# Cross-attention and routed attention: the high part of the routed rows written by VectorE, the product repeated on GpSimd

## The reference

```
x = x + xattn(layernorm(x), ctx)                  # 8 heads, 77 context rows
rw = gating(layernorm(x))                         # 16 weights per token
q, k, v = sum_e rw[t, e] * (x @ {q,k,v}_proj[e])
attn = softmax(causal(q k^T / 8)) v
mixed = attn[:, :, None, :] * rw[..., None]
x = x + einsum('bted,edc->btc', mixed, o_proj)
```

## Time and profile before

| | |
|---|---|
| median of 3 runs | 2802.98 us |
| the profiled execution's own time | 2805.71 us |
| its span, first to last instruction | 2803.8 us |
| busy share of the span: PE, PEld, DVE, ACT, POOL | 96%, 92%, 87%, 36%, 42% |
| mean granted TensorE clock | 0.991 |

### The profile page before, as it was taken

How to read it: one execution, slowest core, us unless ns; L and a number is a source line. 1 busy time by engine, 2 the same in 40 slices (tenths; PEclk the granted TensorE clock), 3 DMA queues, 4 the chain that set the end, 5 groups by cost and what they waited for, 6 DMA issues and landing times.

```text
span 2803.8 us, 64494 instructions
## 1 busy us (share of the span) xinstructions
PE 2702.4 (96%) x19012; PEld 2581.8 (92%) x19012; DVE 2439.1 (87%) x6755; ACT 1020.0 (36%) x2448; POOL 1190.0 (42%) x1739
## 2 busy tenths in 40 slices
PE   5999999999999999999999999999999999999996
PEld 4999999999999999999999999999999999999996
DVE  6898888888888888988988889888889889888884
ACT  3343333333333333433333333333334334333331
POOL 1343443444444434434434434444344344344343
PEclk8999999999999999999999999999999999999998
DMA  4111111111111111111111111111111111111111
GB/s 103 29 45 44 32 44 35 40 44 28 44 48 28 44 44 31 44 44 31 44 39 36 44 30 41 48 28 44 44 31 44 44 31 44 43 32 44 35 36 39
DMA packets 131435, 113.58 MB, mean 41 GB/s; under 512 B 24720, under 2 KB 130640, under 8 KB 131408
## 3 DMA queue, kind: packets, MB, share of 16 engines
q1 hardware_dynamic: 131408, 113.23, 16.5%
HBM read 95.38 MB, written 17.83 MB: 40 GB/s over the span
## 4 chain that ended last, share of the span: by engine, by line
PE 73%; DVE 12%; issue 9%; ACT 4%; POOL 1%; DVEq 1%; POOLq 0%; DMA 0%; ACTq 0%; SPq 0%
PE bank_b L373 9%; PE bank_b L374 8%; PE bank_a L375 8%; PE bank_b L375 8%; PE bank_a L374 8%; PE bank_a L373 8%; PE bank_c L373 4%; PE bank_c L375 4%; PE bank_c L374 4%; PE bank_a L485 4%; DVE acc L996 3%; DVE acc L993 2%; DVE mix L1037 1%; PE bank_a L445 1%; DVE s_max L923 1%
## 5 line engine op out<-in xcount | busy, mean ns | idle before, releaser
L373 PE MATMUL bank_b<-wqkv_hi,x2T_lo 128*128 128x384 f32 (+1 forms) x2048 | 726.4, 355 | 34.3 <-DVE acc L996 33.7
L374 PE MATMUL bank_b<-wqkv_lo,x2T_hi 128*128 128x384 f32 (+1 forms) x2048 | 693.5, 339 | 0.0
L375 PE MATMUL bank_b<-wqkv_hi,x2T_hi 128*128 128x384 f32 (+1 forms) x2048 | 688.8, 336 | 0.0
L996 DVE SCALAR_TENSOR_TENSOR acc<-bank_b,rw,acc 128x192 f32<-128x192 f32 x1792 | 641.6, 407 | 5.3 <-PE bank_b L375 2.9
L1252 POOL TENSOR_TENSOR mixs_lo<-mix,mixs_hi 128x512 fp32r<-128x512 f32 x256 | 379.9, 1514 | 153.7 <-ACT mixs_hi L772 153.7
L373 PEld LDWEIGHTS bank_b<-wqkv_hi,x2T_lo 128*128 128x128 f32 x2048 | 385.8, 188 | 57.5 <-DVE acc L996 53.6
L374 PEld LDWEIGHTS bank_b<-wqkv_lo,x2T_hi 128*128 128x128 f32 x2048 | 386.2, 189 | 0.0
L375 PEld LDWEIGHTS bank_b<-wqkv_hi,x2T_hi 128*128 128x128 f32 x2048 | 385.1, 188 | 0.0
L1174 POOL TENSOR_TENSOR pow_out<-pow_in,expo 128x2 f32<-128x2 f32 (+1 forms) x128 | 111.7, 873 | 596.4 <-DVE pow_in L853 509.3
L373 PE MATMUL bank_c<-wo_hi,mixs_lo 128*128 128x256 f32 x1024 | 293.9, 287 | 3.7 <-POOL mixs_lo L1252 3.7
L375 PE MATMUL bank_c<-wo_hi,mixs_hi 128*128 128x256 f32 x1024 | 288.0, 281 | 0.0
(11 more groups left out here) (196 smaller groups left out, 6991.1 us busy)
## 6 DMA issues: line engine op xcount, KB each, us to landing
rw_all<-rw_dram SPq DMA_DIRECT2D x128, 512.0 KB, 5.7
xt<-in_x_dram SPq DMA_DIRECT2D x64, 256.0 KB, 2.7
out_dram<-mix SPq DMA_DIRECT2D x64, 256.0 KB, 2.2
ct<-in_ctx_dram SPq DMA_DIRECT2D x64, 57.8 KB
ct<-in_ctx_dram SPq DMA_DIRECT2D x64, 19.2 KB
mix<-in_L_ffn_o_proj_dram SPq DMA_DIRECT2D x2, 512.0 KB, 4.2
rw_dram<-rwT SPq DMA_DIRECT2D x64, 16.0 KB, 1.4
x_tiles<-in_L_xattn_Wq_dram SPq DMA_DIRECT2D x1, 512.0 KB, 6.9
```

Source lines behind the costliest of these rows:

```text
L373: nc.tensor.matmul(dst, lhs[1], rhs[0], start=start, stop=False)
L374: nc.tensor.matmul(dst, lhs[0], rhs[1], start=False, stop=False)
L375: return nc.tensor.matmul(dst, lhs[0], rhs[0], start=False, stop=stop)
L996: V.scalar_tensor_tensor(acc[:, t, k, :], src, rw[:, t, e:e + 1], acc[:, t, k, :], ALU.mult, ALU.add).then_inc(b_evac, 1)
```

## The change

DVE writes the product straight into the rounded tile `mixs[0]`, so that its output is the high part. ACT's copy goes. POOL makes the same product again, in float32, into `mix`, waits for its own product and for DVE's, and subtracts as before. The semaphores follow: `mix_ready` is now POOL's, `mix_hi` is DVE's; SP's reload of `rw_all` and ACT's next write of `aT2` wait for both readers; DVE waits, before it overwrites `mixs[0]`, for the last output product of the batch before; the wait for the store of `y` moves from DVE to POOL.

```diff
--- before.py
+++ after.py
@@ -326,6 +326,7 @@
                 sp.wait_ge(rwT_out, 16 * (n + 1))
                 if not (known(n) and n == 0):
                     sp.wait_ge(mix_ready, at(4, n - 1, 3))
+                    sp.wait_ge(mix_hi, at(4, n - 1, 3))
                 for k in range(2):
                     sp.dma_start(rw_all[k * D:(k + 1) * D, :, :],
                                  rw_dram[:, :].rearrange("(a k) t -> k a t", k=2)[k].partition_broadcast(D)).then_inc(rw_all_in, 16)
@@ -765,11 +766,10 @@
 
             def c_pv(n):
                 act.wait_ge(c_fill, c_at(n, C_PV))
+                if not (known(n) and n == 0):
+                    act.wait_ge(mix_ready, at(4, n - 1, 3))
+                    act.wait_ge(mix_hi, at(4, n - 1, 3))
                 nc.scalar.activation(aT2[:, :], bank_c(C_PV)[:, 0:T], copy).then_inc(aT2_ready, 1)
-
-            def c_mix(n, j):
-                act.wait_ge(mix_ready, at(4, n, j))
-                nc.scalar.activation(mixs[0][:, 2 * j:2 * j + 2, :], mix[:, 2 * j:2 * j + 2, :], copy).then_inc(mix_hi, 1)
 
             def step(i):
                 ahead, now, before, earlier = i + 1, i, i - 1, i - 2
@@ -779,7 +779,6 @@
                         fn(n, *k)
                         later(split_weights, fn.__name__.replace("exp", "s"), n, *k)
 
-                do(earlier, c_mix, 3)
                 do(now, a_exp, 1)
                 do(now, a_exp, 2)
                 do(now, a_exp, 3)
@@ -804,10 +803,7 @@
                 do(now, b_exp)
                 do(before, c_pT)
                 do(before, c_pv)
-                do(before, c_mix, 0)
                 do(ahead, a_exp, 0)
-                do(before, c_mix, 1)
-                do(before, c_mix, 2)
 
             for i in range(-1, 3):
                 step(i)
@@ -1032,10 +1028,10 @@
             def c_mix(n, j):
                 dve.wait_ge(rw_all_in, 32 * (n + 1))
                 dve.wait_ge(aT2_ready, at(1, n, 0))
-                if j == 3 and not (known(n) and n == 0):
-                    dve.wait_ge(y_out, 16 * n)
-                V.tensor_tensor(mix[:, 2 * j:2 * j + 2, :], rw_all[:, 2 * j:2 * j + 2, :],
-                                aT2[:, :].unsqueeze(1).to_broadcast([P, 2, T]), ALU.mult).then_inc(mix_ready, 1)
+                if j == 0 and not (known(n) and n == 0):
+                    dve.wait_ge(c_fill, c_at(n - 1, C_Y))
+                V.tensor_tensor(mixs[0][:, 2 * j:2 * j + 2, :], rw_all[:, 2 * j:2 * j + 2, :],
+                                aT2[:, :].unsqueeze(1).to_broadcast([P, 2, T]), ALU.mult).then_inc(mix_hi, 1)
 
             def c_y(n):
                 dve.wait_ge(c_fill, c_at(n, C_Y))
@@ -1248,6 +1244,13 @@
                                 ALU.mult).then_inc(p_ready, 1)
 
             def c_mix(n, j):
+                pool.wait_ge(rw_all_in, 32 * (n + 1))
+                pool.wait_ge(aT2_ready, at(1, n, 0))
+                if j == 3 and not (known(n) and n == 0):
+                    pool.wait_ge(y_out, 16 * n)
+                G.tensor_tensor(mix[:, 2 * j:2 * j + 2, :], rw_all[:, 2 * j:2 * j + 2, :],
+                                aT2[:, :].unsqueeze(1).to_broadcast([P, 2, T]), ALU.mult).then_inc(mix_ready, 1)
+                pool.wait_ge(mix_ready, at(4, n, j))
                 pool.wait_ge(mix_hi, at(4, n, j))
                 G.tensor_tensor(mixs[1][:, 2 * j:2 * j + 2, :], mix[:, 2 * j:2 * j + 2, :],
                                 mixs[0].bitcast(F32)[:, 2 * j:2 * j + 2, :], ALU.subtract).then_inc(mix_lo, 1)
```

## The result

| | before | after |
|---|---|---|
| median of the runs | 2803.93 us (4 runs, 2802.65 to 2807.08) | 3137.93 us (4 runs, 3137.86 to 3139.62) |
| span of the profiled execution | 2803.8 us | 3137.8 us |
| mean granted TensorE clock | 0.991 | 0.956 |

The ratio is 1.119, 95% interval 1.117 to 1.121: 334 us slower. The forecast was 3086 us with a range of 3010 to 3175.

The account below looks back on a forecast made before the run. PE, busy 96%, was taken as the bound, with POOL just in time for it. 276 us for 62 steps plus 2 and 5 at the end gave 283 us on the 2803.0 median: 3086 us, range 3010 to 3175.

Parts of the forecast that it names:

- POOL's chain sets the transposes: POOL's products, own waits and subtractions form one strict chain ahead of `a_p`, whose transposes PE then starts late.
- The chain's length: From `aT2` to POOL's last subtraction: eight instructions of 1.30 us, own waits and DVE's turns, 12.55 us instead of 7.75.
- rival 2: POOL's multiply is cheaper than `a_xb`, 1.01 us for 512 elements: 69 us less, 3017 us; chance 0.07.
- The transposes 4.45 us later: PE starts `a_pT` 0 at 1449.2 instead of 1444.72; the step pays all of it.
- rival 1: Granted clock falls in PE's new stops, some 3 us each: 3273 us every step, 3149 one in three; chance 0.2.
- The steps: The 62 steps in which mixes are followed by an `a_p` each pay 4.45 us: 276 us.
- The ends: The last two mixes, with no `a_p` behind them: 5 us in the last step, 2 us in the one before.
- The signs: POOL idle below 0.5 us before the mix, PE waiting 4 to 5 us for POOL, step about 47 us.
- The sign for rival 1: A granted clock below 0.95 in the steady steps would show that the clock falls in PE's stops.
- Waits and the rounded write costed at nothing: New waits of SP, ACT, DVE and POOL cost nothing; DVE's rounded write keeps the same 692 ns.
- rival 3: Not slower: POOL's chain ends within 8.1 us, in time for `a_pT`, 2803 us; chance 0.02.
- rival 4: DVE takes fewer turns against POOL than laid out: up to 1.4 us less per step, 2999 us; chance 0.04.

## Why the prediction was right, point by point

**POOL's chain sets the transposes: right, and measured from both sides.** Taking the product out removes all of the loss, halving it leaves 89 us.

**The chain's length: 12.55 us forecast, 12.28 seen.** The product on POOL alone takes 1.28 to 1.31 us, as the row of `a_xb` said, so rival 2 (a multiply of 1.01 us) is out, and so is the estimate of 1.11 us by the Trainium skill, page "GPSIMD Engine Reference", section 3.1. The order of turns came out as laid out; only the wait for DVE's first two products was split, 0.70 us ahead of POOL's first subtraction and 0.3 within it, which took 1.58. DVE's turns cost 1.65 us, where I had 1.95; that is the difference.

**The transposes 4.45 us later: 4.41 seen**, by 15.19 against 10.78 us. Some 0.2 of these are the clock (the last two pairs of quarter 1 at half rate), so the chain alone is 4.2.

**The clock: the term that was missing from the sum.** I kept the clock at its level in the forecast and gave its fall 0.2. It falls in every step but the third, so the event of rival 1 came, at a third of its price: the level of 1.2 GHz lasts some 3.4 us ((1.00 - 0.59) and (1.00 - 0.55) of two us each, over 0.50), not 7. Some 0.4 us of it lie in the stop itself. The last two pairs of quarter 1 take 1.44 us instead of 0.71, but with the stops filled PE waits 0.2 us for `a_p` at this place and starts the transposes only 0.2 us sooner, so only 0.2 of that counts. The transposes pay 0.78. Together that is 1.0 us, and by the run with the stops filled 0.9 per step, 58 us in all, where rival 1 had 186 for every step.

My reading of the earlier trace rows was the weak point. I put the new stretch between one of 0.52 and one of 0.82 us of work in two. But the 0.7 us were over 3.3 us, which is thinner than both; and what came was 0.97 us of work in the two us ahead of the fall, more than in the row of 0.82, behind which the clock had stayed up. So the work in two us did not sort these cases.

**The range: met in part by luck.** I drew its upper end for a fall in one step of three at 3 us each. It fell in nearly all of them at 0.9, and the sum stayed inside. The forecast was 3086 us; the chain makes 14 less, the clock 58 more, the ends 3 and the first steps 3 more, together 3136; measured 3138.

**The steps: 62 x 4.45 = 276 forecast.** Seen are 5.17 us a step, so 320 us in 62, of which 262 are the chain and 58 the clock.

**The ends: 7 us forecast, 10 seen.** The last `a_xb` starts at 3030.14 and the span ends 107.7 us later, 92.2 before; an ordinary step's 5.2 off, that is 10.3. Some 3 us more came in the first steps, which differ between kernels of this series by as much (39 to 42 us for the second).

**The signs.** Near the mark: POOL's groups at 1401 and 1435 ns, ACT's group gone, DVE's product at 1167 ns, a step of 47.8 us. Missed: POOL's idle time ahead of the mix is 0.66 us, not below 0.5. PE's listed waits for POOL are 2.2 us per step, all for `mixs_lo`, and not 4 to 5 with `probs` among them: 1.03 us of the delay shows as waits for DVE, more of it is not listed, and the slow pairs fill the wait for `probs`, which is there with 0.2 us in the run with the stops filled. The sign for rival 1, a clock below 0.95 in the steady steps, did not go off at 0.96 although the clock fell in them: a mean over the step was too coarse a sign.

**Waits and the rounded write costed at nothing: right.** SP's, ACT's and DVE's new waits show in no list, and the kernel without the product holds those on `mix_hi` and DVE's own and is faster than before. DVE's product from PSUM takes 677 ns written rounded (L1034) and 677 ns in float32 (L1036).

**DVE: not costed, hidden.** PE's waits for DVE grow from 0.55 to 1.03 us per step (0.68 and 0.35 in the step shown). They lie ahead of POOL's stops and cost nothing of their own, as forecast: with the stops filled, taking DVE's waits away too made the step shorter by what POOL's chain lost, 1.65 us, and by no more.

**Not slower (rival 3), and DVE taking fewer turns (rival 4):** neither came. POOL's chain ran 12.1 us from its first instruction (1598.57 to 1610.71) where rival 3 needed 8.1, and DVE's turns were 1.65 of them, against 10.49 us with the product from PSUM; rival 4 would have left as little as 0.55.

## What to carry to other kernels

An engine that is idle for more than half of the time can still be the next bound: ask how long the chain is between the result that releases it and the consumer that needs it, and count every added instruction into that chain at full length, less the idle time at its head that it fills. When two engines stand still for each other over SBUF operands, moving one operand to PSUM where it already lies may be worth more than moving the work. And where the bound is PE, a stop costs more than its listed length, since the matmuls around it no longer overlap, and it can cost the clock behind it as well.

## What the runs showed of the hardware that I had not expected

In the changed kernel the granted clock fell from 1.00 to 0.50 in a stop of 1.61 us that followed one of 0.59 us, with about 1.0 us of matmuls between them, and eleven small matmuls in each stop kept it at 1.00. With DVE's product from PSUM stops of the same 0.58 and 1.60 us made it fall in some steps and not in others.

The rows read as if DVE and POOL took turns as whole instructions when both read two operands from SBUF: DVE's 0.68 us becomes 1.1, and up to 1.77, POOL's 1.28 becomes 1.6 to 1.78. With one of DVE's operands in PSUM neither shows any effect: 677 ns, and 1283 to 1292.
